# Expert rows scattered batch by batch into fixed regions, and expert weights waited for one expert at a time

## What is computed

```python
x = x + windowed_self_attention(layernorm(x), W)             # window of 64
x = x + cross_attention(layernorm(x), ctx_768, mask)         # 8 heads of 64, 77 keys
h = layernorm(x)
top1 = argmax(h @ router_w + router_b)                       # one of E = 8 experts for each of the 4096 rows
x = x + gelu(h @ W1[top1] + b1[top1]) @ W2[top1] + b2[top1]  # W1 (8,256,1024), W2 (8,1024,256)
# second layer: RWKV mixing, cross-attention with top-32, state-space model, feed-forward, ternary linear
```

## Time and profile before

| | |
|---|---|
| median of 3 runs | 1920.25 us (1919.13 to 1920.98) |
| profiled execution, its own time | 1922.16 us |
| profiled execution, span from first to last instruction | 1920.5 us |
| PE busy | 1642.0 us, 85% of the span |
| DVE busy | 1310.4 us, 68% |
| ACT busy | 864.1 us, 45% |
| POOL busy | 655.7 us, 34% |
| bytes moved by DMA | 92.91 MB |

### The profile page before, as it was taken

The page is one execution under the profiler, slowest core; times in us unless marked ns, Lnnn a source line. Parts: engine busy times, 40 slices in busy tenths (PEclk is TensorE's granted clock), DMA queues, the critical chain, the costliest instruction groups (busy, mean ns, idle before and its releaser), DMA issues.

```text
span 1920.5 us, 26433 instructions
## 1 busy us (share of the span) xinstructions
PE 1642.0 (85%) x7946; PEld 1260.9 (66%) x7946; DVE 1310.4 (68%) x4214; ACT 864.1 (45%) x1714; POOL 655.7 (34%) x1016
## 2 busy tenths in 40 slices
PE   5899999983299999992679999999999999998765
PEld 3677777772166767762557777777777777776543
DVE  3567777762158778434477888889888888986642
ACT  1444444440031111114556766677766667764231
POOL 1112222213400000005534556555545655543221
PEclk9899999995599999995888999999999999999777
DMA  9000000005744343325000000000000000000000
GB/s 270 7 1 1 1 1 1 1 1 206 281 136 137 98 128 105 113 94 183 6 6 6 12 6 12 12 6 12 12 12 7 12 6 7 7 6 7 1 6 11
DMA packets 81060, 92.91 MB, mean 48 GB/s; under 512 B 19142, under 2 KB 69527, under 8 KB 80667
## 3 DMA queue, kind: packets, MB, share of 16 engines
q1 hardware_dynamic: 72235, 77.73, 12.6%
q0 software_dynamic: 3072, 8.39, 1.3%
q10 hardware_dynamic: 5616, 5.11, 0.8%
HBM read 70.76 MB, written 20.45 MB: 47 GB/s over the span
## 4 chain that ended last, share of the span: by engine, by line
PE 25%; DVE 12%; ACT 11%; issue 4%; POOL 2%; DMA 0%; ACTq 0%; DVEq 0%; POOLq 0%
PE E_pK L2177 3%; PE E_pU L2318 3%; PE E_pY L2165 3%; PE E_pK L2218 3%; PE E_pS L2281 3%; PE E_pY L2328 2%; DVE E_wk L1748 2%; ACT E_mixB L1930 2%; PE E_pU L2290 1%; PE E_pY L2177 1%; ACT E_mix L1930 1%; ACT E_ex L2040 1%; PE E_pY L2228 1%; PE E_pT L2159 1%; DVE E_m L1741 1%
## 5 line engine op out<-in xcount | busy, mean ns | idle before, releaser
L1226 ACT ACTIVATE F_uT<-F_puT 128x512 f32<-128x512 f32 x78 | 42.7, 595 | 285.5 <-PE F_puT L1287 254.4
L1498 POOL TENSOR_SCALAR E_var<-E_mv 128x2 f32<-128x2 f32 x80 | 40.6, 507 | 310.1 <-DVE E_mv L1617 309.6
L1277 PE MATMUL F_pu<-C_W,F_hT 128*128 x312 | 144.1, 606 | 1.3 <-issue 1.3
L1297 PE MATMUL F_py<-C_W,F_uT 128*128 x624 | 141.2, 379 | 0.5 <-ACT F_uT L1226 0.5
L2318 PE MATMUL E_pU<-E_xT,E_W 128*128 128x256 f32 x512 | 122.2, 395 | 12.4 <-ACT E_xT L2067 12.4
L1297 PEld LDWEIGHTS F_py<-C_W,F_uT 128*128 128x128 f32 x624 | 115.6, 190 | 15.3 <-issue 1.2
L2228 PE MATMUL E_pY<-E_Wcv,E_hid 128*128 128x256 f32 x512 | 118.2, 385 | 3.9 <-issue 2.5
L2318 PEld LDWEIGHTS E_pU<-E_xT,E_W 128*128 128x128 f32 x512 | 100.0, 198 | 31.8 <-ACT E_xT L2067 17.7
L2328 PE MATMUL E_pY<-E_W,E_hid 128*128 128x256 f32 x512 | 115.6, 379 | 0.0
L2218 PE MATMUL E_pK<-E_cmix,E_Wck 128*128 128x256 f32 x512 | 115.3, 379 | 0.0
L2228 PEld LDWEIGHTS E_pY<-E_Wcv,E_hid 128*128 128x128 f32 x512 | 96.0, 192 | 28.7 <-issue 16.6
(11 more groups left out here) (408 smaller groups left out, 4304.8 us busy)
## 6 DMA issues: line engine op xcount, KB each, us to landing
F_b<-in_L_ffn_b SPq DMA_DIRECT2D x39, 512.0 KB, 4.4
C_W<-in_L_ffn_W SPq DMA_DIRECT2D x16, 1024.0 KB
sorted_x<-zero SPq DMA_DIRECT2D x1, 4992.0 KB, 19.8
F_xs<-sorted_x SPq DMA_DIRECT2D x39, 128.0 KB, 2.4
F_b<-in_L_ffn_b SPq DMA_DIRECT2D x39, 128.0 KB, 3.1
sorted_y<-F_y ACTq DMA_DIRECT2D x39, 128.0 KB, 2.4
out<-E_tB SPq DMA_DIRECT2D x16, 256.0 KB, 2.1
X<-in_x SPq DMA_DIRECT2D x3, 1024.0 KB, 10.6
```

What stands on the lines that cost most here:

```text
L1277: last = nc.tensor.matmul(p_u[:, f, :], hT[:, i % 2, kb, :], W1[:, bass.ds(e, 1), kb, f * 512:(f + 1) * 512], start=kb == 0, stop=kb == KD ...
L1297: last = nc.tensor.matmul(p_y[:, 0:D], uT[:, f, :], W2[:, bass.ds(e, 1), f, :], start=f == 0, stop=f == FB - 1)
```

## The change

Each expert gets a fixed region of 4096 rows (B*S) in `sorted_x`, which becomes 32768 x 256 instead of 4992 x 256. A row's address is then expert * 4096 + its rank among the rows of that expert, which is known as soon as its own batch and those before it are routed. So the attention pipeline keeps a running one-hot sum (`seen`), TensorE makes the ranks of a batch with two small matmuls (`ranks`), VectorE picks them (`number_rows`), and GpSimd scatters the batch's two groups of rows in a later iteration. The loops of VectorE and TensorE get one more iteration, that of GpSimd two more. The zeros now cover the whole tensor of 33.6 MB, in eight transfers. `place_rows` keeps the small sums that give `place`, `owner`, and for each block the row of `sorted_x` where it begins (`source`), which SyncE reads into a register ahead of each load of rows. The weights of experts 0 to 2 are loaded from ScalarE's queue in `place_rows`, those of experts 3 to 7 from the same queue in the first blocks, each pair behind the store of a block; each expert has a semaphore of its own, and `first(i)` waits for that of expert i only (every expert gets at least one block, so block i never needs an expert beyond i).

```diff
+            for e in range(E):
+                sp.dma_start(xs_dram[e * B * S:(e + 1) * B * S].rearrange("(p b) d -> p (b d)", p=P)
+                             .rearrange("p (c z) -> p c z", z=P),
+                             k["zero"][:].unsqueeze(1).to_broadcast([P, B * S * D // P // P, P])).then_inc(ld["zeroed"], 16)
+            sp.wait_ge(ld["zeroed"], 16 * E)
...
+            LATER = {7: (0, 1), 8: (2, 3)}
+
+            def scatter(i):
+                pool.wait_ge(r["target"], i + 1)
+                if i == 0:
+                    pool.wait_ge(ld["zeroed"], 16 * E)
+                for n in (2 * i, 2 * i + 1):
+                    nc.gpsimd.indirect_dma_start(
+                        out=xs_dram, out_offset=bass.IndirectOffsetOnAxis(ap=target[:, n:n + 1].bitcast(U32), axis=0),
+                        in_=X[:, n, :], in_offset=None).then_inc(scattered, 16)
...
-            for n in range(B + 3):
+            for n in range(B + 5):
...
                     add_bo(n - 1)
+                for i in LATER.get(n, (n - 5,) if 9 <= n < B + 5 else ()):
+                    scatter(i)
...
+            def count(i):
+                dve.wait_ge(r["hot"], i + 1)
...
+                ve.tensor_tensor(seen[:, 2 * i + 1, :], seen[:, 2 * i, :], hot[:, 2 * i, :], ALU.add).then_inc(r["seen0"], 1)
+                dve.wait_ge(r["seen0"], i + 1)
+                ve.tensor_tensor(seen[:, 2 * i + 2, :], seen[:, 2 * i + 1, :], hot[:, 2 * i + 1, :],
+                                 ALU.add).then_inc(r["seen"], 1)
+
+            def number_rows(i):
+                dve.wait_ge(r["rkp"], i + 1)
+                for t in range(2):
+                    last = ve.tensor_tensor_reduce(picked[:, 2 * i + t, :], p_turn[:, 0, (2 + t) * E:(3 + t) * E], hot[:, 2 * i + t, :],
+                                                   1.0, 0.0, ALU.mult, ALU.add, rank[:, 2 * i + t:2 * i + t + 1])
+                last.then_inc(r["rk"], 1)
+                dve.wait_ge(r["rk"], i + 1)
+                ve.scalar_tensor_tensor(out=target[:, 2 * i:2 * i + 2], in0=atf[:, 2 * i:2 * i + 2], scalar=float(B * S),
+                                        in1=rank[:, 2 * i:2 * i + 2], op0=ALU.mult, op1=ALU.add).then_inc(r["target"], 1)
...
+                if 0 <= n - 4 < B:
+                    count(n - 4)
                 if 0 <= j < B:
                     scores(j, 0)
...
                     choose(n - 3)
+                if 0 <= n - 4 < B:
+                    number_rows(n - 4)
                 if 0 <= q < B:
                     apply_R(q)
...
+            def ranks(i):
+                pe.wait_ge(r["hT"], min(i + 2, B))
+                pe.wait_ge(r["seen"], i + 1)
+                pe.wait_ge(ld["tri"], 1)
+                tiles = slice(2 * i, 2 * i + 2)
+                to = p_turn[:, 0, 2 * E:4 * E]
+                te.matmul(to, tri[:], hot[:, tiles, :].rearrange("p n e -> p (n e)"), start=True, stop=False)
+                te.matmul(to, ones[:], seen[:, tiles, :].rearrange("p n e -> p (n e)"), start=False,
+                          stop=True).then_inc(r["rkp"], 1)
...
             def turn_B(i):
                 pe.wait_ge(b["h"], i + 1)
                 past(pe, r["lg"], i - 3)
+                past(pe, r["rk"], i - 4)
                 turn(p_turn, hB).then_inc(b["hTp"], 1)
...
+AHEAD = 3
+def load_expert(engine, args, W1, W2, loaded, e):
+    engine.dma_start(W1[:, e], args["L0_ffn_W1"][e].rearrange("(k p) f -> p k f", p=P)).then_inc(loaded[e], 16)
+    engine.dma_start(W2[:, e], args["L0_ffn_W2"][e].rearrange("(k p) d -> p k d", p=P)).then_inc(loaded[e], 16)
...
+        @block.scalar
+        def _(act):
+            for e in range(AHEAD):
+                load_expert(act, args, W1, W2, loaded, e)
...
-            pool.wait_ge(c["place"], 2)
-            for n in range(NT):
-                nc.gpsimd.indirect_dma_start(
-                    out=xs_dram, out_offset=bass.IndirectOffsetOnAxis(ap=place[:, n:n + 1].bitcast(U32), axis=0),
-                    in_=X[:, n, :], in_offset=None).then_inc(c["scattered"], 16)
-            pool.wait_ge(c["scattered"], 16 * NT)
...
         def load_xs(engine, i):
+            at = engine.value_load(source[0:1, i:i + 1], min_val=0, max_val=E * B * S - P)
             past(engine, s["y"], i - XB)
-            engine.dma_start(xs[:, i % XB, :], xs_dram[i * P:(i + 1) * P]).then_inc(dma[f"xs{i % XB}"], 16)
+            engine.dma_start(xs[:, i % XB, :], xs_dram[bass.ds(at, P)]).then_inc(dma[f"xs{i % XB}"], 16)
...
+            sp.wait_ge(scattered, 16 * NT)
             for i in range(3):
                 load_xs(sp, i)
...
                 gelu(i)
                 store(i - 1)
+                if i - 1 + AHEAD < E:
+                    load_expert(act, args, W1, W2, loaded, i - 1 + AHEAD)
...
                 pe.wait_ge(s["hT"], i + 1)
+                if i < E:
+                    pe.wait_ge(loaded[i], 32)
...
             turn_rows(0)
             turn_rows(1)
-            pe.wait_ge(loaded, 32 * E)
             first(0)
```

More of the change, by code:

```diff
@@ L818, in _ @@
             nc.vector.tensor_scalar(owner[:], ownerf[:], float(E - 1), None, ALU.min).then_inc(c["owner"], 1)
-            dve.wait_ge(c["owner"], 1)
+            step(nc.vector.tensor_reduce(sourcef[:], skipped[:, :, 0:E - 1], AX.X, ALU.add))
+            nc.vector.scalar_tensor_tensor(out=source[:], in0=number_b[:, :, 0], scalar=float(P), in1=sourcef[:],
+                                           op0=ALU.mult, op1=ALU.add).then_inc(c["owner"], 1)
+            step(nc.vector.tensor_tensor(row[:], hot[:], start[:].unsqueeze(1).to_broadcast([P, NT, E]), ALU.mult))
@@ L821, in _ @@
+            step(nc.vector.tensor_reduce(placef[:], row[:], AX.X, ALU.add))
+            nc.vector.tensor_tensor(place[:], placef[:], sent["rank"][:], ALU.add).then_inc(c["place"], 1)
+            dve.wait_ge(c["place"], 1)
+            dve.wait_ge(c["owner"], 2)
         @block.tensor
         def _(pe):
-            pe.wait_ge(c["tri"], 1)
-            every = hot[:].rearrange("p n e -> p (n e)")
-            nc.tensor.matmul(p_in[:, 0:NT * E], tri[:], every, start=True, stop=True).then_inc(c["counts_in"], 1)
@@ L826, in _, with expert_blocks @@
-            nc.tensor.matmul(p_tot[:, 0:NT * E], ones[:], every, start=True, stop=True).then_inc(c["counts_tot"], 1)
-def expert_blocks(nc, args, k, owner, xs_dram, ys_dram, W1, W2, loaded, E, F, BLOCKS, X, ahead, lw, folded_film,
+            nc.tensor.matmul(p_tot[:, 0:E], sent["ones"][:], sent["seen"][:, NT, :], start=True,
+                             stop=True).then_inc(c["counts"], 1)
+def expert_blocks(nc, args, k, owner, source, xs_dram, ys_dram, W1, W2, loaded, scattered, E, F, BLOCKS, X, y, ahead, lw, folded_film,
```

108 lines of the change are left out of this document (52 added, 56 removed).

## The result

Over 20 runs each, the median went from 1920.24 us to 1911.68 us (1908.41 to 1919.95), and the means stand at a ratio of 0.9963 (95% interval 0.9952 to 0.9974). The change makes the kernel faster, as predicted, but by 8.6 us and not by 26, and the time lies above the range of 1883 to 1908. The profiled execution took 1909.09 us with a span of 1907.2 us. In the rows PE is TensorE (PEld its weight loads), DVE VectorE, ACT ScalarE and POOL GpSimd; SPq and ACTq are the transfers that SyncE and ScalarE issue.

The account below looks back on a forecast made before the run. The prediction saw 67.1 us between the last routing decision and the first expert matmul, filled by the scatter beside 16.8 MB of weights. An earlier first matmul (-32.3 us) and weight waits (+6) gave -26.3 us: 1894 us, range 1883 to 1908.

Parts of the forecast that it names:

- Attention: Attention loop up to the last one-hot: the new picks, counts and ranks add 5.0 us, one-hot ready at 455.2.
- a late `turn_B`: Attention iterations 4 to 15: turn_B waits for number_rows, 0.25 us each reaching the critical cycle, 3.0 us in all.
- The last batches: Attention's drain: 0.5 us for number_rows and 0.3 for ranks; afterwards GpSimd's last scatter ends at 461.1.
- The step between the blocks: From attention's last scatter to placing: 3.25 us, as from 450.19 to 453.44 in the kernel before.
- The placing: place_rows: ScalarE's six weight transfers set the end after 8.1 us, at 472.4, and at 475.7 with the barrier.
- The first rows: Start of expert blocks: register read 1.04 us, then 7.21, plus 1 for weights still moving; first matmul at 484.9.
- The weights: Experts 3 to 7: first(3) waits 3 to 4.6 us, first(6) 2, others hardly; sum 6 us, bounds 0 and 12.
- the second rival: First eight blocks: weights bound them, 14 us a pair, waits of 6.6 + 3.2 + 6.6 us, TensorE at half clock; 1905 us, 13%.
- The fit of the Trainium skill: Weights of experts 3 to 7: 2.0 us plus bytes over 436 GB/s, a pair landing in 6.8 us, none late.
- The second layer: After the expert stage: the second layer stays as it was.
- the zeros: Before the first scatter: 33.6 MB over by 180 us, TensorE as busy beside them; rival that they come late, 3%.
- GpSimd's scatters in the loop: Attention loop: costed at nothing; up to 2.6 us in all if scatters block VectorE in iterations 7 and 8.

Follow-up runs that it names:

- e1: Changed kernel with VectorE doing number_rows ahead of choose instead of behind it: 1910.82 us, ratio 0.9941 to the kernel before.
- e9: Changed kernel with the edits of e1, e4 and e5 together: 1890.51 us, ratio 0.9831 to the kernel before.
- e11: e9 with the later side loads of e8 added: 1889.71 us, ratio 0.9807 to the kernel before.
- e6: Kernel before with only a semaphore for each expert's weights, scatter and weight issue unchanged: 1919.77 us, ratio 1.0000.
- e12: e11 with ScalarE waiting for the first three blocks' rows before issuing the weights of experts 2 and 3: 1892.43 us, ratio 0.9855 to the kernel before.
- e5: Changed kernel with the last two batches' four scatters moved from attention into placing: 1903.23 us, ratio 0.9919 to the kernel before.
- e3: Changed kernel loading the two film matrices for 16 of 128 partitions only: 1912.91 us, ratio 0.9950 to the kernel before.
- e8: Changed kernel with film and kernel loads and the steps that follow from them three blocks later: 1902.64 us, ratio 0.9900 to the kernel before.
- e7: Changed kernel with all eight experts' weights issued in placing (AHEAD = 8): 1922.46 us, ratio 1.0001 to the kernel before.
- e4: Changed kernel issuing two experts' weights in placing, three around the first gelu, expert i+4 in block i: 1902.57 us, ratio 0.9885 to the kernel before.

## Why the prediction was wrong, step by step

At the stage's end the sum said -26.3 us and the profile shows -6.0. The 20 us are these:

- **Attention, +5.0 predicted, +9.1 measured** (last one-hot ready at 459.28). The mechanism and the wait were right (0.22 us against 0.25, `turn_B` released by VectorE), and `count` and `ranks` cost less than their 1.2. The step that failed is the claim that a late `turn_B` costs its delay and no more: TensorE's clock fell for a part of four iterations, 5.0 us. Without the wait these four are gone in e1, e9 and e11; that such falls also come without it (e6, e12) leaves open how much of the 5 us is the wait's alone. The last batches cost 1.6 us where 0.8 stood in the sum.
- **The last batches.** GpSimd ended at 464.67, 5.4 us behind the one-hot where 5.9 was the sum: right. **The step between the blocks, 3.25 predicted, 5.7 measured.** It was taken from a barrier that no indirect DMA stood ahead of; e5 moved the 5.7 us along with the scatters.
- **The placing, 8.1 and 3.25 + 1.04 predicted, 8.6 and 1.85 measured.** ScalarE's fifth issue sets the end, as predicted (473.63, 4.18 us). At this block's end the barrier and the register read together cost less than the read's row and the attention's barrier in sum.
- **The first rows, 7.21 + 1 predicted, 11.5 measured.** The step "1 us more because the weights are still moving" was mis-sized: the rows took 6.4 us instead of 2.1 to land, at a DMA share of 1.06. e12 shows that this is company on the engines.
- **The weights, 6 predicted (0 to 12), 18.4 measured.** Expert 3 was late as predicted, but by 8.2 us instead of 3 to 4.6, because its pair landed after 15.8 us and not 10 to 12: that landing time is the term of the sum that failed most. Expert 6 was late by 0.8 (2 was said), and expert 7, which was to wait hardly at all, by 2.9. The waits sum to 12.0, the bound's very end. What the sum left out is in the second rival: behind both long waits TensorE did part of its product at half clock, 1.9 + 1.6 us, and the first block lost 0.7. (A long wait doesn't always bring this: in e3 the product behind a wait of 3.3 us took 3.70.) The last 2 us fell in later blocks. So this rival, which had 13%, named the mechanism, and it gave 1905 for it. The fit of the Trainium skill (DMA: Bandwidth & Descriptors, the anatomy of one DMA), by which a pair lands in an estimated 6.8 us, stands there for transfers that GpSimd issues, and these are ScalarE's. It holds for no pair of the changed kernel: beside a second busy queue the same bytes took 15.8 us, the pair of expert 6 took 8.2, and in e8 that of expert 3 took 11.3 with the side loads gone.
- **The second layer, no change predicted**: it was 7.3 us shorter in this pair of profiles and the same or longer in others. In all fourteen profiles the short layer goes with a granted clock of 0.84 to 0.87 in the 13 us from 142 us behind the stage's end, and the long one with 0.50 to 0.56. That this also spreads the 20 runs, eleven from 1908 to 1913 and nine from 1915 to 1920, is likely and not shown, since one of them has a profile. What it gave back in the median is luck, and no part of the sum.

Right were the direction; the zeros, which cost the attention beside them nothing in this pair of profiles (they fill the DMA engines in the first three slices, and the 60.8 us of the loop from the transposes of `A_hA` at 102.5 to those of `A_prA` at 163.3 took 60.6 us, from 102.9 to 163.5; the other profiles with these zeros reach the first point between 102.2 and 105.2, so that up to 2.7 us ahead of it aren't excluded in them); that neither part works alone (e6, e7); and that GpSimd's scatters in the loop hardly hold VectorE. For that the Trainium skill (SBUF — State Buffer, the rules for kernel authors) has the rule that a two-port operation of VectorE, or one with both inputs in SBUF beside a GpSimd operation that reads SBUF, and one of GpSimd block each other. One place of e1 shows a hold that the rule as stated doesn't reach: in the iteration with four scatters the addition on scores, for which VectorE was free at 234.62 and TensorE's `A_ps` done at 234.45, starts 0.03 us after the last scatter's end. The page gives such an addition no two-port mode, and one of its inputs is in PSUM, while the 8-column additions of `count`, with both inputs in SBUF, ran beside the scatter.

```profile
234.22 0.96 POOL L252 DMA_INDIRECT sorted_x<-X,A_target  x1 [0.30 <-issue]
...
234.45 0.17 DVE L395 TENSOR_TENSOR C_shared<-C_shared 128x8 f32<-128x8 f32 x1
...
235.21 0.86 DVE L337 TENSOR_TENSOR A_scB<-A_ps,A_bias 128x308 f32<-128x308 f32 x2 [0.59 <-PE A_ps L670]
```

It cost 0.6 us, once, where up to 2.6 were feared, and the same in e9 and e11. In e12 the same addition came 1.4 us late, 0.8 us behind the scatter's end, so what holds it stays open.

## What to carry to other kernels

Work that moves off a long serial stage leaves the loads that were hidden under it bare: before summing the gain, list what was issued early there (16.8 MB of weights), and give each load its new issue time and its landing under the traffic then, taken from the fullest stretch and not from a transfer alone. A wait of 0.25 us more on TensorE may bring a fall of its clock with it, so put new work of another engine ahead of the operation that TensorE already waits for, not behind it. And give the issues of large transfers to the engine only as many at a time as the next stage needs: e4's stage ends 15.8 us ahead of the change's, and its median is 9 us lower, with the same transfers in another order.

## What the hardware showed unexpectedly

- The end of a stage that an indirect DMA of GpSimd stands ahead of takes 5.7 us from that instruction's end (470.39 - 464.67, and the same in seven experiments); without one the same end took 2.9 us (e5).
- 128 KB of rows landed 2.1 us after their issue with idle DMA engines (before, 510.04), 3.1 in e12, 5.3 to 6.4 beside weights, and 12 us with film loads of 1.5 MB and 640 KB of biases ahead on their own queue (e4).
- TensorE, idle 0.66 us ahead of `turn_B` in each iteration and busy nine tenths of it, kept its full clock in some iterations and did 1.99 us of matmuls in 3.01 in others. With 0.33 us of idle there it did the same matmuls in 2.74 and 2.87 us, twice in e12 and not at all in e1, e9 and e11.
- In the second layer, a stretch with TensorE 100% busy has a granted clock of 0.50 to 0.56 for 13 us in nine profiles and 0.84 to 0.88 in five, and the layer is 3 to 11 us longer with the first. None of these runs was made to settle what decides it.
